# Weighted sums: the layout of the expanded blocks, of the transposed weights, and of the operand that the final products stream

## The chip, the cores and the metric

The kernel runs on one core of a Trainium2 chip. The metric is the time of one execution on the device in microseconds (us). The median of three runs is 10403.76 us (10387.06 to 10404.04).

## What is computed

Inputs are x and ctx of shape (32, 128, 1024) in fp32: 32 batch elements, 128 channels, 1024 points. Four layers follow one another. The first three are attention layers (chunked, with LoRA projections, chunked again); they give x3. The fourth finds, for each of the 1024 points, its 30 nearest neighbours among the points given by the first three channels of ctx, turns relative coordinates into features, sends these through a small network of three layers with batch norm, and ends so:

```
att = softmax(h[..., 0], axis=-1)                 # (B, 1024, 30)
xk  = x.transpose(0, 2, 1)[bidx, idx]             # rows of the 30 neighbours
agg = einsum('bnkc,bnk->bnc', xk, att)            # weighted sum of 30 rows
return x + agg.transpose(0, 2, 1)
```

(here C is 128). The change touches only the computation of `agg`.

## The kernel before

Most of the program is a loop over the 32 batch elements (attention layers, neighbour search, coordinates), followed by the network over all points. After that comes the stage of the weighted sums, again a loop over the 32 batch elements i. Within it every engine runs its own list of instructions, written out by hand, and semaphores alone order them against one another.

The stage gathers nothing. The weight with which source point m enters target point n is built as a product of one-hots. The index of a neighbour, 0 to 1023, is split by GpSimd into a high part l (0 to 15) and a low part (0 to 63), m = 64 l + low. There are 120 rows (4 groups of 30 neighbours) on the partitions and 256 columns of target points. Per batch element:

- `normalise` (L1451, VectorE) scales the attention; `transposes` (L753, TensorE) puts it into PSUM with the 120 rows on partitions.
- `weights` (L1463, VectorE), twice: for each l, BA[l] = (high part == l) times attention, an array of 16 x 128 per half.
- `blocks` (L1053, ScalarE), four times four operations: the expansion. For j = 0 to 3 it copies a quarter of BA, 1024 elements, into BD, scaled by `blockmask[:, j]`, which is 1 on the 30 rows of group j and 0 elsewhere. It runs in the order (h, p, l): it reads BA in steps of 128 elements (512 bytes), l innermost.
- `onehots` (L1472, VectorE), eight times: A1 = (low part == 0..63), 2048 elements.
- `chunk` (L766, TensorE), eight times: 32 products, each A1 (120 x 64, stationary) against 64 columns (l, j) of BD, into the PSUM buffer SCA or SCB. An fp32 product is two matmul records in the trace, so a chunk is 64 records.
- `columns` (L1061, ScalarE), eight times: the eviction of SCA or SCB, 128 x 1024, into WT, the transposed weights of half a batch element.
- `final` (L779, TensorE), twice: for each l and each half h of the partitions a product of X3D (64 x 128, stationary; rows of x3, loaded from DRAM) with the 256 columns (c, j) of WT at that l, accumulated over the 16 values of l in the PSUM bank PD (h = 0) or MISC (h = 1). Again 64 records.
- `finish` (L1486, VectorE) adds x3 and the result goes out over SyncE's queue.

BD, A1, SC, WT and X3D have two buffers each. The order on the engines: TensorE runs chunks 0 and 1, the second final of batch element i - 1, the transposes of i + 1, chunks 2 to 5, the first final of i, and chunks 6 and 7. ScalarE runs for v = 0 to 3 the blocks for the next pair of chunks, then the columns of chunks 2v and 2v + 1. VectorE runs one-hots 0 and 1, weights(1), one-hots 2 and 3, finish(i - 1), one-hots 4 and 5, weights(0) of i + 1, one-hots 6 and 7. A chunk waits for its one-hots (`a_done`), its blocks (`bd_done`) and the eviction of the chunk two before (`wt_done`). A one-hot waits for the chunk two before, since it overwrites its A1 (`chunk_ready`). `final` waits for the four evictions of its half.

The layouts before, innermost index last: BD is (h, p, l, j), so for one j the expansion writes in steps of 4 elements (16 bytes). The columns of a chunk's products are (l, j). WT is (l, c, j): the eviction reads PSUM straight and writes runs of 4 elements, and the 256 columns of one l lie side by side.

Of the kernel before, what the change touches and what calls it, by code (L numbers as in the profile page):

```python
# [25 lines left out]
GROWS = 4 * KNN  # L26
# [5 lines left out]
def program(nc, x_in, ctx_in, mask_in, w_in, b_qkv, w_out, wq, wk, wv, wo, at, bq, bk, bv, bo,  # L32
            mlp_k, consts, out, NB=B):
    f32, u32, bf16 = mybir.dt.float32, mybir.dt.uint32, mybir.dt.bfloat16
    ALU, ACT, AX = mybir.AluOpType, mybir.ActivationFunctionType, mybir.AxisListType
# [14 lines left out]
    with stack:  # L50
        def sb(name, shape, dt=f32):
            return stack.enter_context(nc.sbuf_tensor(name, shape, dt))

        def sem(name):
            return stack.enter_context(nc.semaphore(name))
# [24 lines left out]
        reg = sb("reg", [P, 3 * T + V1W + V2W])  # L80
# [50 lines left out]
        blockmask = con[:, 400:404]  # L131
# [17 lines left out]
        def pb(name, n):  # L149
            return stack.enter_context(nc.psum_tensor(name, [P, 512 * n], f32))  # L150
        SC = [pb("SCA", 2), pb("SCB", 2)]
# [44 lines left out]
        chunk_ready, wt_done, fin_ready, out_done = (sem(n) for n in (  # L196
            "chunk_ready", "wt_done", "fin_ready", "out_done"))
# [19 lines left out]
        def load_part(eng, q):  # L217
# [4 lines left out]
        LV, HV = 16, 64  # L222
        UC = 64
        free = arena[:, B * PAIRS:]
        BD = [free[0:GROWS, n * UC * 64:(n + 1) * UC * 64].rearrange("r (h p l j) -> r h p l j", h=2, p=32, l=LV)
              for n in range(2)]
        WT = [w.rearrange("p (l c j) -> p l c j", l=LV, j=4) for w in (free[:, 8192:12288], reg[:, 0:4096])]
        X3D = [w.rearrange("p (l c) -> p l c", l=LV) for w in (free[:, 12288:14336], kexp[:, :])]
        A1 = [gat[0:GROWS, n * 2048:(n + 1) * 2048].rearrange("r (h p c) -> r h p c", h=2, p=16) for n in range(2)]
        BA = [w[0:GROWS, :].rearrange("r (l c) -> r l c", l=LV) for w in (S01, pd01)]  # L230
# [30 lines left out]
        def settle(eng):  # L261

            eng.sem_inc(waited, 1)
# [164 lines left out]
        def _(pe):  # L428
# [3 lines left out]
            for n, (W, kc, w) in enumerate(WCHUNKS):  # L432
                if n >= 2:
                    pe.wait_ge(lora_done, n - 1)
                for c in range(0, w, 512):
                    last = mm(SC[n % 2][:, c:min(c + 512, w)], A_OF[id(W)][:, kc * P:(kc + 1) * P],
                              B_OF[id(W)][:, c:min(c + 512, w)], start=True, stop=True)
# [3 lines left out]
            for n in range(2):  # L441
                last = mm(MISC[:, n:n + 1], WL[n][:, 384:512], bL[:, n, 2:3], start=True, stop=True)
# [52 lines left out]
            with pe.Fori(0, NB) as i:  # L495
# [119 lines left out]
                for c in range(2):  # L615
                    for kc in range(KC):
                        last = mm(SC[1][:, c * P:(c + 1) * P], Wk[:, kc, c * P:(c + 1) * P], ctxT[:, kc, :],
                                  start=(kc == 0), stop=(kc == KC - 1))
                last.then_inc(k_ready, 1)
                for kc in range(KC):  # L620
                    last = mm(SC[1][:, 512:768], ctxT[:, kc, :], Wv[:, kc, :], start=(kc == 0), stop=(kc == KC - 1))
# [3 lines left out]
                for kc in range(KC):  # L625
                    last = nc.tensor.transpose(TP[:, kc * P:(kc + 1) * P], X1[:, kc * P:(kc + 1) * P], ident)
                last.then_inc(hT_ready, 1)
                pe.wait_ge(hT_evac, i + 1)
                for c in range(KC):
                    for kc in range(KC):  # L630
                        last = mm(SC[0][:, c * P:(c + 1) * P], Wq[:, kc, c * P:(c + 1) * P], hT[:, kc, :],  # L631
                                  start=(kc == 0), stop=(kc == KC - 1))
# [27 lines left out]
                for h in range(2):  # L660
                    for c in range(KC):
                        last = mm(SC[0][:, h * 512:(h + 1) * 512], OT[:, c * P:(c + 1) * P],  # L662
                                  Wo[:, c, h * 512:(h + 1) * 512], start=(c == 0), stop=(c == KC - 1))
# [7 lines left out]
                for t in range(NT):  # L671
                    last = nc.tensor.transpose(TP[:, t * P:(t + 1) * P], X0[:, t * P:(t + 1) * P], ident)
# [53 lines left out]
            with pe.Fori(0, NCH // 2 - 1) as i:  # L726
                for u in range(2):
                    n = i * 2 + u
# [9 lines left out]
            with pe.Fori(0, PARTS) as i:  # L738
                for u in range(PCH // 2):
                    n = i * (PCH // 2) + u  # L740
                    pe.wait_ge(a2_done, n + 1)
                    pe.wait_ge(h3_done, n + 1)
                    for h in range(2):
                        last = mm(SC[u % 2][0:G, h * CW:(h + 1) * CW], k3, act2[u % 3][0:GR, h * CW:(h + 1) * CW],
                                  start=True, stop=True)
# [11 lines left out]
            def chunk(i, c):  # L757
                v = c // 2
                pe.wait_ge(a_done, i * 8 + c + 17)
                if c % 2 == 0:  # L760
                    pe.wait_ge(bd_done, i * 4 + v + 5)
                pe.wait_ge(wt_done, i * 8 + c + 1)
                settle(pe)
                for p in range(16):
                    for h in range(2):
                        last = mm(SC[c % 2][64 * h:64 * h + 64, p * 64:(p + 1) * 64], A1[c % 2][:, h, p, :],  # L766
                                  BD[v % 2][:, h, c % 2 * 16 + p, :, :].rearrange("r l j -> r (l j)"),
                                  start=True, stop=True)
                last.then_inc(chunk_ready, 1)

            def final(i, par, k, half):
                pe.wait_ge(wt_done, i * 8 + 4 * half + 6)
                if half == 0:
                    pe.wait_ge(x3T_ld[par], k * 32 + 32)
                    pe.wait_ge(out_done, i + 2)
                settle(pe)
                for l in range(LV):
                    for h in range(2):
                        last = mm(FIN[h][:, half * 256:(half + 1) * 256], X3D[par][64 * h:64 * h + 64, l, :],  # L779
                                  WT[half][64 * h:64 * h + 64, l, :, :].rearrange("p c j -> p (c j)"),  # L780
                                  start=(l == 0), stop=(l == LV - 1))
                last.then_inc(fin_ready, 1)

            def aggregate(i, par, k, first=False, last=False):
                chunk(i, 0)
                chunk(i, 1)
                if not first:
                    final(i - 1, 1 - par, k - 1 + par, 1)
                if not last:
                    transposes(i + 1, 1 - par)  # L790
                for c in range(2, 6):
                    chunk(i, c)
                final(i, par, k, 0)
                chunk(i, 6)
                chunk(i, 7)
                if last:
                    final(i, par, k, 1)
# [13 lines left out]
        def _(act):  # L811
            A = nc.scalar.activation
# [35 lines left out]
            with act.Fori(0, NB) as i:  # L848
                if True:
# [90 lines left out]
                    for j in range(2):  # L940
                        last = A(halves[:, :, j, :], SC[1][:, 0:256].rearrange("p (c t) -> p c t", c=2), ACT.Copy,
                                 scale=pairmask[:, j:j + 1])
# [55 lines left out]
            with act.Fori(0, NCH // 2) as i:  # L998
                for u in range(2):
                    n = i * 2 + u  # L1000
                    act.wait_ge(l1_ready, n + NCH + 1)
                    act.wait_ge(l2_ready, n + 1)
                    for h in range(2):
                        last = A(S[u][0:GR, h * CW:(h + 1) * CW], SC[u][0:GR, h * CW:(h + 1) * CW], ACT.Identity,
                                 scale=gain[0:GR, h:h + 1], bias=shift[0:GR, h:h + 1])
# [41 lines left out]
            def blocks(i, v):  # L1047
                half, w = v // 2, v % 2
                act.wait_ge(ba_done, i * 2 + half + 5)
                act.wait_ge(chunk_ready, i * 8 + 2 * v + 2)  # L1050
                src = BA[half].rearrange("r l (h p) -> r h p l", h=2)[:, :, 32 * w:32 * w + 32, :]
                for j in range(4):
                    last = A(BD[v % 2][:, :, :, :, j], src, ACT.Copy, scale=blockmask[0:GROWS, j:j + 1])  # L1053
                last.then_inc(bd_done, 1)

            def columns(i, c):
                half = c // 4
                act.wait_ge(chunk_ready, i * 8 + c + 5)
                if c % 4 == 0:
                    act.wait_ge(fin_ready, i * 2 + half + 3)  # L1060
                A(WT[half][:, :, c % 4 * 16:c % 4 * 16 + 16, :].rearrange("p l c j -> p c l j"),  # L1061
                  SC[c % 2][:, :].rearrange("p (c l j) -> p c l j", l=LV, j=4), ACT.Copy).then_inc(wt_done, 1)

            def aggregate(i, last=False):
                for v in range(4):
                    if v < 3:
                        blocks(i, v + 1)
                    elif not last:
                        blocks(i + 1, 0)
                    columns(i, 2 * v)  # L1070
                    columns(i, 2 * v + 1)

            act.sem_inc(bd_done, 4)
            act.sem_inc(wt_done, 2)
            blocks(0, 0)
            with act.Fori(0, NB - 1) as i:
                aggregate(i)
# [520 lines left out]
```

## Time and profile before

| | |
|---|---|
| median of the runs | 10403.76 us |
| the profiled execution | 10408.93 us |
| its span, first to last instruction | 10407.0 us |
| busy: TensorE matmul | 7886.3 us (76%) |
| busy: VectorE | 7988.5 us (77%) |
| busy: ScalarE | 4010.1 us (39%) |
| busy: GpSimd | 511.4 us (5%) |
| mean granted TensorE clock | 0.764 of full speed |
| L1053, expansion | 512 operations, 534.9 + 538.0 us busy |
| L1472, one-hots | 256 operations, 583.0 us busy |

The shares are means over stages with different limits; what a change of one stage is worth has to be read inside that stage. In the groups the busy time of a line is a union in time, since operations of an engine overlap a little; the mean of one is from its start to its end. Idle time is shown with what released it. "reg", "arena", "kexp", "gat" are big SBUF tensors in which the arrays named above lie: BD in arena, WT in arena (first half) and reg (second half), A1 in gat, BA in S (first half) and pd (second half), X3D in arena and kexp.

### The profile page before, as it was taken

What the parts mean: (1) busy time and instruction counts of PE and PEld (TensorE: products, weight loads), DVE (VectorE), ACT (ScalarE), POOL (GpSimd) and SP (SyncE); (2) the same over time, 40 slices, a digit from 0 to 9 for tenths busy, and PEclk for the clock granted to TensorE, in tenths of its full rate; (3) what the DMA queues carried; (4) which work ended last, traced back from release to release, by engine and by line L of the source; (5) the groups of instructions that cost most, each with busy time, mean ns of one, the idle gap of its engine ahead of it and who ended that gap; (6) DMA issues with size and microseconds to landing.
All of it is one profiled execution on the core that took longest, in us unless ns stands there. A gap on an engine that the chain in (4) does not pass through costs nothing.

```text
span 10407.0 us, 195918 instructions
## 1 busy us (share of the span) xinstructions
PE 7886.3 (76%) x79424; PEld 5345.1 (51%) x79424; DVE 7988.5 (77%) x11226; ACT 4010.1 (39%) x4783; POOL 511.4 (5%) x776
## 2 busy tenths in 40 slices
PE   7777777777777777777777777777777775778888
PEld 4444444554544444545444444555554542277777
DVE  6887777788777877877777787787888785766666
ACT  2333333333233333333332332333332220499999
POOL 0000000000000000000000000000000000010000
PEclk8777777777777777777777777777777777889899
DMA  2111111111111111111111111111111113122222
GB/s 80 45 45 42 45 42 44 44 42 45 45 45 45 45 45 45 45 45 42 45 42 42 43 44 45 44 44 45 45 45 35 44 43 82 37 52 62 54 62 49
DMA packets 325409, 487.83 MB, mean 47 GB/s; under 512 B 133378, under 2 KB 246162, under 8 KB 323826
## 3 DMA queue, kind: packets, MB, share of 16 engines
q1 hardware_dynamic: 238269, 371.72, 11.6%
q10 hardware_dynamic: 86197, 102.55, 3.3%
q8 instruction: 712, 11.67, 0.5%
q14 instruction: 231, 1.89, 0.1%
HBM read 401.33 MB, written 72.88 MB: 46 GB/s over the span
## 4 chain that ended last, share of the span: by engine, by line
PE 46%; DVE 25%; ACT 15%; issue 12%; DMA 1%; DVEq 0%; ACTq 0%; SPq 0%; POOL 0%; POOLq 0%
ACT arena L1053 6%; PE PD L465 5%; PE PD L466 5%; PE SCA L662 5%; DVE m L1207 4%; PE SCA L631 3%; DVE pd L1213 3%; PE MISC L490 3%; PE TP L654 3%; PE SCA L506 2%; ACT S L859 2%; DVE mx L1258 2%; PE SCB L506 2%; DVE S L1252 2%; ACT kexp L892 2%
## 5 line engine op out<-in xcount | busy, mean ns | idle before, releaser
L1207 DVE MAX8 m<-pd 128x8 f32<-128x1024 f32 x1024 | 1251.2, 1222 | 316.4 <-ACT pd L834 160.5
L1211 DVE FIND_INDEX8 idx<-m,pd 128x8 uint32<-128x1024 f32 x1024 | 1248.4, 1219 | 9.6 <-issue 9.6
L506 PE MATMUL SCA<-con,S 128*128 128x128 f32 x1536 | 317.4, 374 | 1120.7 <-ACT S L859 1120.7
L1213 DVE MATCH_REPLACE8 pd<-m,pd 128x1024 f32<-128x1024 f32 x768 | 928.3, 1209 | 0.0
L506 PEld LDWEIGHTS SCA<-con,S 128*128 128x128 f32 x1536 | 249.1, 192 | 1187.7 <-ACT S L859 1187.7
L490 PEld LDWEIGHTS MISC<-ptab,gat 128*128 128x128 bf16 x23400 | 650.9, 101 | 363.6 <-issue 342.4
L1472 DVE TENSOR_TENSOR gat<-maskT,con 120x2048 f32<-120x2048 f32 x256 | 583.0, 2308 | 294.1 <-PE SCA L766 277.2
L465 PE MATMUL PD<-arena 128*128 128x512 f32 x1028 | 774.1, 846 | 43.6 <-ACT pd L834 25.7
L834 ACT ACTIVATE pd<-PD,xxcol 128x512 f32<-128x512 f32 x514 | 352.9, 686 | 1168.5 <-PE PD L466 1168.5
L859 ACT ACTIVATE S<-S 128x1024 f32<-128x1024 f32 x384 | 404.4, 1053 | 841.7 <-DVE S L1259 568.7
L466 PE MATMUL PD<-arena,con 1*128 1x512 f32 x1028 | 727.1, 793 | 0.0
L490 PE MATMUL MISC<-ptab,gat 128*128 128x24 bf16 x23400 | 673.5, 177 | 44.0 <-issue 26.8
L854 ACT ACTIVATE OT<-TP 128x256 f32<-128x256 f32 x384 | 147.1, 383 | 1301.9 <-PE TP L535 1301.9
L1241 DVE RECIPROCAL sm<-TP 128x16 f32<-128x16 f32 (+1 forms) x384 | 91.4, 238 | 620.2 <-PE TP L654 310.6
L506 PE MATMUL SCB<-con,S 128*128 128x128 f32 x1536 | 338.7, 393 | 275.1 <-ACT S L859 275.1
L1053 ACT ACTIVATE arena<-S,con 120x1024 f32<-120x1024 f32 x256 | 534.9, 2256 | 17.9 <-DVE S L1463 17.9
L1131 DVE TENSOR_TENSOR prod<-MISC,hm 128x480 f32<-128x480 f32 x390 | 405.6, 1040 | 173.0 <-PE MISC L490 173.0
L1053 ACT ACTIVATE arena<-pd,con 120x1024 f32<-120x1024 f32 x256 | 538.0, 2277 | 0.0
L662 PE MATMUL SCA<-arena,OT 128*128 128x512 f32 x1024 | 537.6, 691 | 0.0
L631 PE MATMUL SCA<-reg,arena 128*128 128x128 f32 x4096 | 494.3, 286 | 35.6 <-ACT reg L948 35.6
L631 PEld LDWEIGHTS SCA<-reg,arena 128*128 128x128 f32 x4096 | 488.2, 202 | 43.2 <-ACT reg L948 43.2
L766 PE MATMUL SCA<-arena,gat 120*64 120x64 f32 x8192 | 323.6, 248 | 237.5 <-ACT reg L1061 135.2
(260 smaller groups left out, 15328.8 us busy)
## 6 DMA issues: line engine op xcount, KB each, us to landing
gat<-low_scratch SPq DMA_DIRECT2D x396, 640.0 KB, 4.3
arena<-in_ctx ACTq DMA_DIRECT2D x33, 512.0 KB, 3.9
maskT<-in_mask ACTq DMA_DIRECT2D x32, 512.0 KB, 4.9
arena<-in_x ACTq DMA_DIRECT2D x32, 512.0 KB, 4.1
x_scratch<-arena ACTq DMA_DIRECT2D x32, 512.0 KB, 4.7
x3T_scratch<-arena ACTq DMA_DIRECT2D x32, 512.0 KB, 3.8
arena<-x3T_scratch SPq DMA_DIRECT2D x32, 512.0 KB, 7.1
arena<-x_scratch SPq DMA_DIRECT2D x32, 512.0 KB, 9.2
```

The lines of the kernel that those rows point to most:

```text
L465: mm(PD[:, :], ctx[:, t * P:(t + 1) * P], ctx[:, h * 512:(h + 1) * 512], start=True, stop=False)
L466: mm(PD[:, :], ones_row, xxrow[0:1, h * 512:(h + 1) * 512], start=False, stop=True).then_inc(pd_ready, 1)
L490: last = mm(place[:, o:o + 3 * NT], oh[n % NOH][:, kk * 256 + half * P:kk * 256 + (half + 1) * P], ptab[:, part, :, :].rearrange("p c t -> ...
L506: last = nc.tensor.transpose(SC[g % 2][:, b * 512 + j * P:b * 512 + (j + 1) * P], S[g % 2][:, b * 512 + j * P:b * 512 + (j + 1) * P], ident)
L631: last = mm(SC[0][:, c * P:(c + 1) * P], Wq[:, kc, c * P:(c + 1) * P], hT[:, kc, :], start=(kc == 0), stop=(kc == KC - 1))
L662: last = mm(SC[0][:, h * 512:(h + 1) * 512], OT[:, c * P:(c + 1) * P], Wo[:, c, h * 512:(h + 1) * 512], start=(c == 0), stop=(c == KC - 1))
L859: A(S[g % 2], S[g % 2], ACT.Exp, scale=scale).then_inc(exp_done, 1)
L1053: last = A(BD[v % 2][:, :, :, :, j], src, ACT.Copy, scale=blockmask[0:GROWS, j:j + 1])
L1207: step(V.max(m, buf[:, :]))
L1211: last = V.max_index(idx[:, t, 8 * r:8 * r + 8], m, buf[:, :])
L1213: step(V.match_replace(buf[:, :], m, buf[:, :], -3.0e38))
L1472: V.tensor_tensor(A1[c % 2], low[:, :, 16 * part:16 * part + 16].unsqueeze(3) .broadcast_to([GROWS, 2, 16, HV]), iota64[0:GROWS, :].unsque ...
```

## The change

BD becomes (h, p, j, l), and WT becomes (c, j, l). The columns of a chunk's products are then (j, l). The expansion reads as before and writes runs of 16 elements; the eviction reads and writes 1024 elements in one run; `final` takes its 256 moving columns at a step of 16 elements (64 bytes). Numbers of instructions, sizes, waits and their order stay as they are.

```diff
-        BD = [free[0:GROWS, n * UC * 64:(n + 1) * UC * 64].rearrange("r (h p l j) -> r h p l j", h=2, p=32, l=LV)
+        BD = [free[0:GROWS, n * UC * 64:(n + 1) * UC * 64].rearrange("r (h p j l) -> r h p j l", h=2, p=32, l=LV)
               for n in range(2)]
-        WT = [w.rearrange("p (l c j) -> p l c j", l=LV, j=4) for w in (free[:, 8192:12288], reg[:, 0:4096])]
+        WT = [w.rearrange("p (c j l) -> p c j l", l=LV, j=4) for w in (free[:, 8192:12288], reg[:, 0:4096])]
...
-                                  BD[v % 2][:, h, c % 2 * 16 + p, :, :].rearrange("r l j -> r (l j)"),
+                                  BD[v % 2][:, h, c % 2 * 16 + p, :, :].rearrange("r j l -> r (j l)"),
...
-                                  WT[half][64 * h:64 * h + 64, l, :, :].rearrange("p c j -> p (c j)"),
+                                  WT[half][64 * h:64 * h + 64, :, :, l].rearrange("p c j -> p (c j)"),
...
-                    last = A(BD[v % 2][:, :, :, :, j], src, ACT.Copy, scale=blockmask[0:GROWS, j:j + 1])
+                    last = A(BD[v % 2][:, :, :, j, :], src, ACT.Copy, scale=blockmask[0:GROWS, j:j + 1])
...
-                A(WT[half][:, :, c % 4 * 16:c % 4 * 16 + 16, :].rearrange("p l c j -> p c l j"),
-                  SC[c % 2][:, :].rearrange("p (c l j) -> p c l j", l=LV, j=4), ACT.Copy).then_inc(wt_done, 1)
+                A(WT[half][:, c % 4 * 16:c % 4 * 16 + 16, :, :].rearrange("p c j l -> p (c j l)"), SC[c % 2][:, :], ACT.Copy).then_inc(wt_done, 1)
```

Some lines outside the change are also shown below: L1131 multiplies a PSUM operand with `hm`, which it reads in steps of 240 two-byte elements (480 bytes); L1110 subtracts, reading `crd` in steps of 3 elements (12 bytes). L1176 and L1179 are two-input operations on contiguous arrays. L863 and L854 are ScalarE's plain copies from PSUM to SBUF.

## Rows read from the trace of the kernel before

**Rows 1.** Page: busy tenths of TensorE and ScalarE in 40 equal slices:

```profile
PE   7777777777777777777777777777777775778888
...
ACT  2333333333233333333332332333332220499999
```

**Rows 2.** By stretch: length; busy PE, PEld, DVE, ACT, POOL; clock; DMA:

```profile
9500.00:9900.00 400.00, 331.14 (x6419) 304.91 (x6416) 261.42 (x431) 399.16 (x241) 37.01 (x50) 0.91 0.25 58
...
9718.40:9723.00 4.60, 4.18 (x73) 4.03 (x75) 0.99 (x6) 4.60 (x3) 0.00 (x0) 0.50 0.02 7
...
9725.80:9733.00 7.20, 7.20 (x66) 6.20 (x66) 2.29 (x1) 7.20 (x5) 0.00 (x0) 1.00 0.01 2
```

**Rows 3.** Who waited for whom, 9500 to 9900: total us, times, longest:

```profile
PE SCA L766 <- ACT reg L1061: 46.4, 10, 5.1
...
ACT arena L1061 <- PE SCB L766: 0.8, 1, 0.8
```

**Rows 4.** Chain of waits, 9500 to 9900, shares by line:

```profile
by line: ACT arena L1053 43.9%; issue 19.6%; ACT reg L1061 8.2%; PE PD L779 6.9%; ACT arena L1061 6.2%; PE SCA L766 5.8%; PE SCB L766 5.0%; DVE gat L1472 1.7%; DVE S L1463 1.4%; ACTq L1058 0.4%; PE TP L753 0.4%; ACTq L1076 0.2%; PE MISC L77
```

**Rows 5.** Timeline, ScalarE: start, duration, engine, line, what, count, idle before:

```profile
9707.29 1.07 ACT L1061 ACTIVATE reg<-SCA 128x1024 f32<-128x1024 f32 x1
...
9709.15 8.31 ACT L1053 ACTIVATE arena<-S,con 120x1024 f32<-120x1024 f32 x4
...
9717.27 1.05 ACT L1061 ACTIVATE reg<-SCA 128x1024 f32<-128x1024 f32 x1
...
9747.23 1.09 ACT L1061 ACTIVATE reg<-SCA 128x1024 f32<-128x1024 f32 x1
```

**Rows 6.** Timeline, TensorE, 9709 to 9734:

```profile
9709.47 2.09 PE L766 MATMUL SCA<-arena,gat 120*64 120x64 f32 x64
...
9711.39 2.04 PE L766 MATMUL SCB<-arena,gat 120*64 120x64 f32 x64
...
9718.46 2.15 PE L766 MATMUL SCA<-arena,gat 120*64 120x64 f32 x35 [5.04 <-ACT reg L1061]
...
9722.52 3.29 PE L766 MATMUL SCB<-arena,gat 120*64 120x64 f32 x64
...
9725.74 0.48 PE L779 MATMUL PD<-reg,arena 64*128 64x256 f32 x1
...
9732.85 0.44 PE L753 MATMUL TP<-con,OT 128*120 128x128 f32 x2
...
9733.22 2.09 PE L766 MATMUL SCA<-arena,gat 120*64 120x64 f32 x64
```

**Rows 7.** Timeline, VectorE: one-hots (L1472) after chunks:

```profile
9711.72 4.49 DVE L1472 TENSOR_TENSOR gat<-maskT,con 120x2048 f32<-120x2048 f32 x2 [4.67 <-PE SCA L766]
```

**Rows 8.** Groups by shape, ScalarE: busy us, mean ns, idle before:

```profile
L1053 ACT ACTIVATE arena<-S,con 120x1024 f32<-120x1024 f32 x256 | 534.9, 2256 | 17.9 <-DVE S L1463 17.9
...
L863 ACT ACTIVATE ET<-SCA 128x1024 f32<-128x1024 f32 x192 | 196.5, 1023 | 232.5 <-PE SCA L506 232.5
...
L854 ACT ACTIVATE OT<-TP 128x256 f32<-128x256 f32 x384 | 147.1, 383 | 1301.9 <-PE TP L535 1301.9
...
L1061 ACT ACTIVATE reg<-SCA 128x1024 f32<-128x1024 f32 x64 | 69.0, 1078 | 2.5 <-PE SCA L766 2.5
```

**Rows 9.** Groups by shape, VectorE:

```profile
L1131 DVE TENSOR_TENSOR prod<-MISC,hm 128x480 f32<-128x480 f32 x390 | 405.6, 1040 | 173.0 <-PE MISC L490 173.0
...
L1176 DVE TENSOR_TENSOR X<-X 128x480 f32<-128x480 f32 x34 | 22.4, 659 | 1.2
...
L1110 DVE TENSOR_TENSOR OT<-crd,own 128x240 f32<-128x240 f32 x102 | 54.0, 585 | 4.2
...
L1179 DVE TENSOR_TENSOR X<-X,S 128x240 f32<-128x240 f32 x34 | 13.9, 408 | 1.2
```

**Rows 10.** Timeline: first expansions (ScalarE) and last addition (VectorE):

```profile
9111.88 16.23 ACT L1053 ACTIVATE arena<-S,con 120x1024 f32<-120x1024 f32 x8 [17.95 <-DVE S L1463]
...
10403.18 0.68 DVE L1486 TENSOR_TENSOR ET<-MISC,arena 128x512 f32<-128x512 f32 x1
```

## The prediction, made before the changed kernel ran

> **What bounds the kernel now.** I read the page's slices first. In 35 of the 40 slices (260 us each) the kernel runs parts that this change does not touch; in the last five, from about 9,100 us on, ScalarE's digit is 9 and TensorE's 7 to 8 [rows 1]. That last eighth is the stage of the weighted sums, the only one in which the three edited operations run. The table by stretch then gives ScalarE 399.2 of 400 us busy, TensorE 331 and VectorE 261 [rows 2]. Who waits for whom says the same: TensorE waits 46.4 us (of 400) for ScalarE's evictions at L1061, and ScalarE waits for TensorE hardly at all [rows 3]. The chain of waits has 43.9% of that stretch on L1053, ScalarE's block expansion, and only 6.9% on the final products [rows 4]. So the stage runs at ScalarE's pace, with TensorE at 83% close behind. ScalarE starts it at 9111.88 and the last addition ends at 10403.86 [rows 10].
>
> The pace: the same eviction recurs at 9707.29 and 9747.23, 39.9 us per batch element [rows 5]. Four expansions take 9717.27 - 9709.15 = 8.12 us, 2.03 each, and two evictions 1.86 us, 0.93 each [rows 5]. A batch element has 16 expansions and 8 evictions: 16 x 2.03 + 8 x 0.93 = 39.9 us.
>
> TensorE in the same time: chunk to chunk 1.92 us (9709.47 to 9711.39), so a pair of chunks is some 3.9 us; a final product from its first matmul to what follows is 9732.85 - 9725.74 = 7.11 us; the two transposes 0.37 us [rows 6]. Sum: 4 x 3.9 + 2 x 7.1 + 0.4 = 30.2 us. The rest of its 39.9 is waiting, and chunks at the lower clock after a wait: the stretch from 9718.4 was granted 0.50, that is 1.2 GHz, after 5.04 us of idling, and one chunk took 4.1 us there; a final product ran at 1.00 (2.4 GHz) [rows 2, 6].
>
> **The change part by part.**
>
> Expansions (512 in all). Reads stay at 512-byte steps; the writes go from 16-byte steps to runs of 16 elements. A plain ScalarE operation of 1024 elements takes 1.02 us, the expansion 2.26 [rows 8]. Which side costs the extra, the trace does not say for ScalarE, since no other operation of it is stepped. VectorE shows that stepped reads alone cost: L1131 (480-byte steps) takes 1040 ns where 480 plain elements take 659, 0.79 ns more per element; L1110 (12-byte steps) 585 where 240 plain take 408, 0.74 ns more [rows 9]. A plain element costs VectorE (659 - 408)/240 = 1.05 ns, so a stepped one costs 1.8 ns or 1.73 times. On ScalarE, whose plain element costs (1023 - 383)/768 = 0.83 ns [rows 8], this is 1.44 ns by the ratio or 1.8 by the time: an expansion of about 1.5 or 1.9 us where it is 2.03. Outer bounds are 0.9 (only the writes cost) and 2.03 (only the reads). I take 1.7. ScalarE then needs 16 x 1.7 + 8 x 0.88 = 34.2 us per batch element; it is 31 at 1.5, 37.4 at 1.9, and 21.4 and 39.5 at the outer bounds.
>
> Evictions (256). They read PSUM in order before and after; the writes go from runs of 4 to one run. L1061 takes 1078 ns against 1023 for the plain copy [rows 8]: 0.05 us off each, 0.4 us per batch element.
>
> Chunk products: same bytes, same contiguous moving operand of 64 columns. Nothing. The output columns only change order.
>
> Final products (64 of them, each of 64 matmul records of 256 columns). The moving columns go from contiguous to 64-byte steps. This is the part that decides, and the trace has no TensorE row with a stepped moving operand. One is 32 pairs of records, one for each of two banks, side by side: 7.11/32 = 0.22 us a pair [rows 6], 0.87 ns per column. Nearest rows are again the stepped reads of VectorE [rows 9]. If SBUF hands over a stepped word each 1.8 ns whoever asks, a final product takes 7.1 x 1.8/0.87 = 14.7 us; if it is the ratio, 7.1 x 1.73 = 12.3; if TensorE's fetch has slack for four-byte words, 7.1. I take twice, 14.2 us, nearer the first, because TensorE asks for its words faster than VectorE (0.87 ns against 1.05), which leaves it less slack, not more.
>
> One row is at odds with a rule of the Trainium skill, and it matters which holds. L1110 steps by 12 bytes and is slow [rows 9]. "SBUF — State Buffer", section "Door 1: The DMA port swizzle", has 16-byte lines, each of which wants two hits to be read at full speed, and calls fp32 steps up to four elements free; L1110 steps by three, so the rule is too kind. For the final products both speak against the change: a step of sixteen elements meets a new line at every column. The rule names no price for TensorE; as a doubling it would give the same 14.2 us.
>
> New pace. TensorE: 4 x 3.9 + 2 x 14.2 + 0.4 = 44.4 us. Then its chunks without a final product ahead of them wait for VectorE's one-hots: a one-hot may start 0.16 us after chunk c-2 (ended 9711.56, started 9711.72), takes 2.24 [rows 6, 7] and lets chunk c begin about 4.6 us after chunk c-2 began, where 3.9 would do: 0.7 us, and 0.3 more for its partner. Twice per batch element (chunks 4, 5 and the next 0, 1), 2 us. In sum 46.4 us against 39.9. ScalarE's 34 us (or 39.5) and VectorE's 26 [rows 2] lie beside it: its gain is off the path. In the last image the final product after chunk 7 is on the path as before, its doubling already counted. Batch elements: 32. 32 x 6.5 = 207 us. No transfer is made later than its user: with 14-us products the loads that follow a finished product have longer than now.
>
> The profiled execution took 10408.9 us (span 10407.0), 5 us over the median of the three runs, 10403.8. 10408.9 + 207 = 10616; on the median 10,611. I predict **10,610 us**. The case's own range: with 12.3-us products 42.6 us a batch element, 32 x 2.7 = +87, or 10,490 on the median; with 14.7 us 47.4, +240, or 10,644; with room for the waits between the engines 10,470 to 10,690.
>
> **Rivals.**
>
> A. TensorE reads the stepped columns at its usual pace or nearly. For it: at 0.87 ns per column these matmuls spend two cycles of 2.4 GHz on each, so a fetch that could deliver a word per cycle has slack. Against it: VectorE has no such slack to spare even at 1.05 ns a word [rows 9]. Then ScalarE's saving counts, down to TensorE's floor of 30.2 + 1.5 to 2 us, about 32. With an expansion of 1.7 us: 34.2, so -5.7 x 32 = -182: 10,220. With 1.9: 37.4, -80: 10,324. With 1.5 or less: 32, -253: 10,150. This also covers a product slowed by a third (9.5 us): 15.6 + 19 + 0.4 + 2 = 37 us, -93: 10,310. Break-even is 39.9 = 18 + 2F, F = 11 us, 1.55 times today's.
>
> The Trainium skill's "Vector Engine (DVE) Microarchitecture Reference", section "5.2 Measured stream behaviour on trn2", has writes at a small step the dearest (2.5 ns per column against about 1.7 for hops), which speaks for the larger saving; no row here shows stepped writes alone.
>
> B. The reads are the whole price of the expansion, and TensorE doesn't mind its steps. ScalarE still sets the pace at 16 x 2.03 + 8 x 0.88 = 39.5: -0.4 x 32 = -13 us, 10,391. Products at 1.55 times end here as well. No change that can be measured.
>
> C. TensorE pays much more than double, because two row groups read stepped at once: at three times 21.3 us, 15.6 + 42.6 + 0.4 + 2 = 60.6, +662: 11,070. Only the fact that no row excludes it speaks for it.
>
> **How the numbers follow.** Forecast case 0.50, A 0.38, B 0.08, C 0.04. A measurement of this kernel can tell about 0.2% (21 us) from no change. Faster by more: 0.38 (A). Within: 0.08 (B). Slower: 0.50 + 0.04. Both signs hold most of the chance, so the range spans them: from 10,140, below A's floor, to 10,700, above the forecast's upper end; outside are C and the extremes, about 0.1. Given the forecast case alone it is 10,470 to 10,690.
>
> **What would show it.** Right: in the profile after, the pitch of L779's pairs goes from 0.22 to some 0.43 us and a product takes 14 us; ScalarE's share in 9,200 to 10,300 falls from 100% to about 75%, TensorE's rises above 95%; L1053's mean falls from 2.26 to 1.6 to 2.0 us, L1061's to 1.02; TensorE waits for VectorE's one-hots in front of chunks 0, 1, 4 and 5, and no longer for L1061. Wrong: L779's pitch stays at 0.22 (A or B, told apart by L1053's mean), or the columns of L779 slow less than 1.55 times. Anything that moves before 9,100 us would be another cause altogether.

## The result: 3.0% slower, and what the profile after shows

The changed kernel takes 10714.24 us (median of 4, 10709.6 to 10716.11); the kernel before, run beside it, 10403.9 us. The ratio is 1.0301, with a 95% interval of 1.0283 to 1.0319. Measured again later beside other versions it was 1.0301 (1.0284 to 1.0318). So the sign is as forecast and the size is not: I forecast +2.0%, with 10,700 as the upper end of the range.

The slices of the page, against [rows 1]. Before 9,100 us nothing of note moved; the last six slices are the stage of the weighted sums, in which TensorE is now at 9 (8 in the first of them) and ScalarE has fallen from 9 to 7 and 8.

```profile
PE   7777777777777777777777777777777756899999
...
ACT  2333333333333333333233333333333304887787
```

Table by stretch (columns as in [rows 2]): TensorE is now busy 367 of 400 us (331 before), ScalarE 319 (399 before): 92% and 80%. The second row lies in a final product, the third and fourth in the pause and the slow chunk told of below; their clocks are 1.00, 0.86 and 0.50.

```profile
9500.00:9900.00 400.00, 367.05 (x5147) 242.25 (x5149) 206.94 (x347) 319.48 (x194) 29.60 (x40) 0.96 0.20 47
9724.40:9738.30 13.90, 13.90 (x66) 6.53 (x64) 5.53 (x8) 13.90 (x9) 3.70 (x5) 1.00 0.19 47
9742.40:9746.70 4.30, 0.00 (x0) 0.00 (x0) 4.30 (x11) 4.30 (x3) 0.00 (x0) 0.86 0.03 4
9746.70:9751.30 4.60, 3.63 (x63) 3.47 (x65) 1.54 (x8) 4.47 (x3) 0.00 (x0) 0.50 0.01 4
```

The timeline of TensorE, which answers to [rows 6]. A pair of final products starts each 0.43 us (9725.28 to 9725.72; 0.22 before), and a final product takes 9738.33 - 9724.35 = 13.98 us (7.11 before). Chunks are as before, 1.92 us apart where nothing keeps them. One of them waits 0.92 us for its one-hots.

```profile
9714.94 0.43 PE L753 MATMUL TP<-con,OT 128*120 128x128 f32 x2
...
9720.17 2.09 PE L766 MATMUL SCA<-arena,gat 120*64 120x64 f32 x64 [0.92 <-DVE gat L1471]
...
9724.35 0.68 PE L779 MATMUL PD<-arena 64*128 64x256 f32 x1
...
9725.28 0.60 PE L779 MATMUL PD<-arena 64*128 64x256 f32 x1
...
9725.72 0.60 PE L779 MATMUL PD<-arena 64*128 64x256 f32 x1
...
9738.33 2.09 PE L766 MATMUL SCA<-arena,gat 120*64 120x64 f32 x64
...
9746.75 2.15 PE L766 MATMUL SCA<-arena,gat 120*64 120x64 f32 x35 [4.47 <-issue]
9749.82 1.86 PE L766 MATMUL SCA<-arena,gat 120*64 120x64 f32 x29 [0.92 <-issue]
9751.37 3.73 PE L766 MATMUL SCB<-arena,gat 120*64 120x64 f32 x64
...
9769.11 0.43 PE L753 MATMUL TP<-con,OT 128*120 128x128 f32 x2
...
9815.53 0.44 PE L753 MATMUL TP<-con,OT 128*120 128x128 f32 x2
```

The transposes come once in a batch element, so they give the pace: 9815.53 - 9769.11 = 46.4 us, the forecast's number, but 9769.11 - 9714.94 = 54.2 us for the one before. The difference, 7.8 us, is in the three L766 rows of 9746 to 9755. TensorE stands still for 4.47 us and waits for nothing ("issue"), stops once more for 0.92 us after record 35 of the chunk, and runs both chunks at half clock. Such a pause comes 14 times between 9,130 and 10,620 us, 100 us apart, once in two batch elements. TensorE's loop runs 15 times, with two batch elements to a run, so it goes back to its start 14 times. That going back, with the slow chunks after it, is called a turn below. Over these 14 the batch element with the pause takes 52.8 to 54.6 us from transposes to transposes, 53.7 in the mean: a turn costs 7.4 us, and the one above is one of the dearer.

The trace shows what happens in the pause. In it lie two DMA packets of the kind "instruction", 16 KB each; they start at 9742.2 and 9742.7 and have landed at 9743.2 and 9744.9, and TensorE goes on 1.9 us later. A third lands at 9748.5, and the second stop ends 1.3 us after it. The view of DMA queues, 9742 to 9747 (packets, MB, share of the 16 DMA engines' time):

```profile
q8 instruction: 2, 0.03, 4.0%
```

The sum over the stage, from the first chunk to the end of the last addition: before 9120.12 to 10403.86, after 9108.65 to 10707.48, which is 315 us more. 32 x (46.4 - 39.9) = 208 and 14 turns x 7.4 = 104 make 312. The first chunk came 11 us earlier in this execution, through parts that the change does not touch; that is why the spans differ by 304 us only.

Groups by shape, against [rows 8]: the expansion went from 2.26 to 2.12 us, the eviction from 1.08 to 1.03.

```profile
L1053 ACT ACTIVATE arena<-S,con 120x1024 f32<-120x1024 f32 x256 | 518.5, 2115 | 18.0 <-DVE S L1462 18.0
...
L1061 ACT ACTIVATE reg<-SCA 128x1024 f32<-128x1024 f32 x64 | 65.8, 1028 | 80.0 <-PE SCA L766 80.0
```

### The profile page after: what moved, and what is told of

Same layout as the page of the kernel before. It is cut to its first block, busy times and chain, and to the rows that moved or that the text cites. A ratio compares the mean times of both kernels' runs of the same rounds, so it can differ in the third digit from the quotient of the medians.

```text
span 10710.6 us, 195918 instructions
## 1 busy us (share of the span) xinstructions
PE 8267.1 (77%) x79424; PEld 5324.0 (50%) x79424; DVE 7980.8 (75%) x11226; ACT 4009.3 (37%) x4783; POOL 511.4 (5%) x776
## 4 chain that ended last, share of the span: by engine, by line
PE 53%; DVE 27%; issue 11%; ACT 7%; DMA 1%; DVEq 1%; SPq 0%; POOL 0%; ACTq 0%; POOLq 0%
PE PD L779 8%; PE SCA L662 5%; PE PD L465 5%; PE PD L466 5%; DVE m L1206 5%; DVE pd L1212 4%; PE MISC L490 3%; PE SCA L766 3%; PE TP L654 3%; PE SCA L506 2%; PE SCA L631 2%; ACT S L859 2%; DVE mx L1257 2%; PE SCB L506 2%; DVE S L1251 2%
## 5 line engine op out<-in xcount | busy, mean ns | idle before, releaser
L854 ACT ACTIVATE OT<-TP 128x256 f32<-128x256 f32 x384 | 147.2, 383 | 1305.6 <-PE TP L535 1305.6
L1053 ACT ACTIVATE arena<-S,con 120x1024 f32<-120x1024 f32 x256 | 518.5, 2115 | 18.0 <-DVE S L1462 18.0
L1053 ACT ACTIVATE arena<-pd,con 120x1024 f32<-120x1024 f32 x256 | 521.6, 2120 | 0.0
L598 PE MATMUL TP<-reg,ET 128*64 128x34 f32 x8192 | 370.6, 255 | 167.0 <-DVE on L1241 167.0
```

The source lines that it names most:

```text
L1053: last = A(BD[v % 2][:, :, :, j, :], src, ACT.Copy, scale=blockmask[0:GROWS, j:j + 1])
```

## Experiments

### TensorE's part undone, ScalarE's kept (e1)

```diff
 # against the changed kernel
-        WT = [w.rearrange("p (c j l) -> p c j l", l=LV, j=4) for w in (free[:, 8192:12288], reg[:, 0:4096])]
+        WT = [w.rearrange("p (l m) -> p l m", l=LV) for w in (free[:, 8192:12288], reg[:, 0:4096])]
...
-                                  WT[half][64 * h:64 * h + 64, :, :, l].rearrange("p c j -> p (c j)"),
+                                  WT[half][64 * h:64 * h + 64, l, :],
...
-                A(WT[half][:, c % 4 * 16:c % 4 * 16 + 16, :, :].rearrange("p c j l -> p (c j l)"), SC[c % 2][:, :], ACT.Copy).then_inc(wt_done, 1)
+                A(WT[half][:, :, c % 4 * 64:c % 4 * 64 + 64],
+                  SC[c % 2][:, :].rearrange("p (m l) -> p l m", l=LV), ACT.Copy).then_inc(wt_done, 1)
```

> The changed kernel with only its TensorE part undone: the expansion reads in steps and writes runs of 16, chunk columns are (j, l), but the eviction reads PSUM in steps of 16 elements (64 bytes) and writes WT as (l, c, j), so the final products stream contiguous columns again. My theory: the slowdown is all TensorE's stepped columns, and the expansion's price lies in its reads. Then the pairs of final products are back at 0.22 us (product 7.1 us), L1053 stays at about 2.12 us mean, and ScalarE sets the pace: 16 x 2.02 + 8 x e, where e is the eviction. If stepped PSUM reads are free for ScalarE (e = 0.93) 39.8 us per batch element and 10,400 us; if they cost it as stepped SBUF reads do (e about 1.8) 46.7 us and 10,620. Rival (the slowdown sits in the new expansion or in the order of the chunk columns): the time stays near 10,710 with final products at 7.1 us.

Measured: 0.9984 of the kernel before (0.9973 to 0.9994), 10,367.7 us. Groups by shape of this version from 9,110 us on, with the final products' mean back at 0.38 us, as in the kernel before:

```profile
L1053 ACT ACTIVATE arena<-S,con 120x1024 f32<-120x1024 f32 x248 | 509.2, 2233 | 0.0
...
L779 PE MATMUL PD<-reg,arena 64*128 64x256 f32 x512 | 114.7, 379 | 0.0
...
L1061 ACT ACTIVATE reg<-SCA 128x1024 f32<-128x1024 f32 x64 | 72.8, 1137 | 4.2 <-PE SCA L766 4.2
```

So the whole slowdown goes with the way in which the final products read. Runs instead of steps in the expansion's writes brought next to nothing (2.23 against 2.26 us); the 2.12 of the changed kernel came in a stage in which the other engines had slowed down, which was not taken apart further. Evicting from PSUM at 64-byte steps costs nothing that the stage feels. From its start to its end an eviction is up to 0.1 us longer than before (1137 ns against [rows 8]'s 1078), but from one to the next it is 0.90 us, against 0.92 before; and e3 below, with the same stepped evictions and ScalarE less busy, has them at 1.02 us, as the changed kernel has its straight ones.

### Final products that read four words together (e2)

```diff
 # against the kernel before
-        WT = [w.rearrange("p (l c j) -> p l c j", l=LV, j=4) for w in (free[:, 8192:12288], reg[:, 0:4096])]
+        WT = [w.rearrange("p (c l j) -> p c l j", l=LV, j=4) for w in (free[:, 8192:12288], reg[:, 0:4096])]
...
-                                  WT[half][64 * h:64 * h + 64, l, :, :].rearrange("p c j -> p (c j)"),
+                                  WT[half][64 * h:64 * h + 64, :, l, :],
...
-                A(WT[half][:, :, c % 4 * 16:c % 4 * 16 + 16, :].rearrange("p l c j -> p c l j"),
-                  SC[c % 2][:, :].rearrange("p (c l j) -> p c l j", l=LV, j=4), ACT.Copy).then_inc(wt_done, 1)
+                A(WT[half][:, c % 4 * 16:c % 4 * 16 + 16, :, :].rearrange("p c l j -> p (c l j)"), SC[c % 2][:, :], ACT.Copy).then_inc(wt_done, 1)
```

> The kernel before, but WT is (c, l, j): the eviction is one straight run, and the final products take their 256 columns in runs of four elements (16 bytes) at steps of 64. Theory: TensorE pays for a single word away from its neighbour, not for a hop, so four together stream at full speed: pair of final products 0.22 us, ScalarE sets the pace with 16 x 2.03 + 8 x 0.88 = 39.5 us, time 10,390. Rival (anything not contiguous halves the stream): pairs at 0.43 us, time near 10,710.

Measured: 0.9999 (0.9987 to 1.0012); final products at 379 to 382 ns mean as before. Hops cost TensorE nothing when four words lie together. The eviction did not get cheaper by being one run (1070 to 1094 ns, 1058 to 1087 before), so the forecast's 0.05 us each was not there in this setting.

### What a step costs TensorE (e7)

```diff
 # against the changed kernel, put in words: columns that a final product streams, by l // 4 (w is the half's 4096 elements)
+half 0: w[0:256], step 2, step 3, step 4
+half 1: step 8, pairs at step 4, pairs at step 32, fours at step 32
```

> The changed kernel with other columns of WT streamed by the final products (so the weighted sums are of wrong numbers; amounts of work are the same): in the first half l = 0-3 contiguous, 4-7 at a step of 2 elements, 8-11 of 3, 12-15 of 4; in the second half l = 0-3 at a step of 8, 4-7 in pairs at a step of 4, 8-11 in pairs at a step of 32, 12-15 in fours at a step of 32. Theory A (a fetch brings 8 bytes, whose two words must both be wanted): 0.22 us a pair of matmuls for contiguous, pairs and fours, 0.43 for every single step of 2 and more. Theory B (16-byte lines, two hits each): step 2 at 0.22, step 3 in between, 4 and 8 at 0.43, pairs 0.22. Theory C (only contiguous is fast): everything else 0.43. The time as such says little: A about 10,500, B about 10,450, C about 10,660.

The timeline of TensorE. Each kind is eight pairs of records; the first block shows where the kinds of half 0 begin (contiguous, 2, 3, 4, and the chunk after), the second those of half 1 (8, pairs at 4, pairs at 32, fours, and the transposes after).

```profile
9738.22 0.48 PE L789 MATMUL PD<-arena,kexp 64*128 64x256 f32 x1
...
9740.05 0.39 PE L789 MATMUL PD<-arena,kexp 64*128 64x256 f32 x1
...
9741.86 0.49 PE L789 MATMUL PD<-arena,kexp 64*128 64x256 f32 x1
...
9744.57 0.62 PE L789 MATMUL PD<-arena,kexp 64*128 64x256 f32 x1
...
9748.30 0.51 PE L767 MATMUL SCA<-arena,gat 120*64 120x64 f32 x10
```

```profile
9719.71 0.70 PE L789 MATMUL PD<-reg,arena 64*128 64x256 f32 x1
...
9723.45 0.40 PE L789 MATMUL PD<-reg,arena 64*128 64x256 f32 x1
...
9725.28 0.37 PE L789 MATMUL PD<-reg,arena 64*128 64x256 f32 x1
...
9727.03 0.37 PE L789 MATMUL PD<-reg,arena 64*128 64x256 f32 x1
...
9728.86 0.43 PE L754 MATMUL TP<-con,OT 128*120 128x128 f32 x2
```

Divided by eight: contiguous 0.23 (0.22 without the start), step 2 0.23, step 3 0.34, step 4 0.47 (0.45 by the starts inside the kind), step 8 0.47; pairs at 4 0.23, pairs at 32 0.22, fours 0.23. That is theory B. Four fp32 words make 16 bytes: 256 words at a step of 3 lie in 192 such lines, 0.34 us or 1.77 ns a line; at a step of 4 in 256, 0.45 us or 1.76 ns; at a step of 2 in 128, which by that price is 0.225 us, about what the words themselves take (0.84 ns each). The step of 16 elements in the changed kernel, 0.43 us or 1.68 ns a line, is a little cheaper than the steps of 4 and 8, which no run takes apart. The time, 10,433 us (one run), is near theory B's 10,450. The rule of the Trainium skill ("SBUF — State Buffer", section "Door 1: The DMA port swizzle": two hits to a 16-byte line for full speed) holds for TensorE with fp32. Its remark that four fp32 elements are a free stride does not: a step of 4 already costs double.

### What a step costs ScalarE (e4 and e8)

```diff
 # e4, against the kernel before; BA's l innermost
-        BA = [w[0:GROWS, :].rearrange("r (l c) -> r l c", l=LV) for w in (S01, pd01)]
+        BA = [w[0:GROWS, :].rearrange("r (c l) -> r c l", l=LV) for w in (S01, pd01)]
...
-                src = BA[half].rearrange("r l (h p) -> r h p l", h=2)[:, :, 32 * w:32 * w + 32, :]
+                src = BA[half].rearrange("r (h p) l -> r h p l", h=2)[:, :, 32 * w:32 * w + 32, :]
...
-                    last = V.scalar_tensor_tensor(BA[half][:, l, :], Lf[par][:, cols], float(l), attT[par][:, cols],
+                    last = V.scalar_tensor_tensor(BA[half][:, :, l], Lf[par][:, cols], float(l), attT[par][:, cols],
```

> The kernel before with BA stored as (c, l) alone: the expansion reads one run and still writes at 16-byte steps. Theory (reads are the whole price and writes are free): L1053 at about 1.05 to 1.2 us, time as for the version that also writes runs, about 0.989 of the kernel before. Rival (a stepped write alone costs as much as a stepped read, and the two hide one another): L1053 stays at about 2 us and the time at that of the kernel before, 0.997 to 1.000 of it.

Measured: 0.9968 (0.9953 to 0.9983), L1053 at 2.22 us. A write at 16-byte steps alone costs nearly as much as both did (1.95 us from one expansion to the next, 2.04 before), and my theory that the writes were free fell.

```diff
 # e8, against the changed kernel, put in words: kinds of expansion by v
+v = 0: run -> step 4;  v = 1: step 2 -> runs;  v = 2: run -> runs;  v = 3: pairs at step 4 -> runs
```

> The changed kernel with four kinds of expansion in turn (the weighted sums are of wrong numbers; the elements moved are as many): v = 0 reads one run and writes at a step of 4 elements; v = 1 reads at a step of 2 and writes runs; v = 2 reads one run and writes runs; v = 3 reads pairs at a step of 4 and writes runs. Theory (16-byte lines, reads only): 1.05 us for v = 0, 2 and 3, and for v = 1, two words to a line, as well. Rival 1 (single words are dear whatever the line): v = 1 at 1.5 to 2.1. Rival 2 (writes cost too): v = 0 at 1.5 to 2.1. The time says nothing here, since TensorE's stepped products set it, about 10,700.

The timeline of ScalarE, the first expansion of each kind, v = 0 to 3:

```profile
9775.17 2.32 ACT L1065 ACTIVATE arena<-S,con 120x1024 f32<-120x1024 f32 x1
...
9738.47 1.23 ACT L1065 ACTIVATE arena<-S,con 120x1024 f32<-120x1024 f32 x1
...
9750.48 1.14 ACT L1065 ACTIVATE arena<-pd,con 120x1024 f32<-120x1024 f32 x1
...
9768.71 1.27 ACT L1065 ACTIVATE arena<-pd,con 120x1024 f32<-120x1024 f32 x1
```

Writes at 16-byte steps cost 2.32 us where runs cost 1.14; reads with two words to a line (1.23, 1.27) are near the full rate. Together with e1 (reads at 512-byte steps, written in runs: 2.23) and the kernel before (both: 2.26): either side at one word to a line sets the pace of about 2 ns an element, and a second one on the other side adds nothing. Rival 2 held. Time: 10,703.7 us, one run, or 1.031 of the kernel before as run beside it; the changed kernel has 1.030. Three quarters of the expansions at about half the price brought nothing: in the changed kernel ScalarE's work is off the path.

### The turn of TensorE's loop (e5)

```diff
-with pe.Fori(0, NB // 2 - 1) as pair:          # 15 turns
-    for odd in (1, 0):
-        aggregate(pair * 2 + (2 - odd), odd, pair + (1 - odd))
+with pe.Fori(0, (NB // 2 - 1) // 3) as trip:   # 5 turns
+    for q in range(3):
+        for odd in (1, 0):
+            aggregate(trip * 6 + (2 * q + 2 - odd), odd, trip * 3 + (q + 1 - odd))
```

> The changed kernel with TensorE's loop over pairs of batch elements written out three pairs to a turn: 5 turns in place of 15, all else the same. In the changed kernel TensorE stands still for about 4.5 us once in two batch elements, with nothing that it waits for, then runs two chunks at the lower clock. Theory: this is the loop's turn, which was hidden when ScalarE set the pace and now costs 54.2 - 46.0 = 8.1 us each time. Ten turns fewer: -81 us, 10,633. Rival (the pause has to do with a wait or with the power throttle, not with the turn): unchanged, 10,700 to 10,715, and the pauses stay 15.

Measured: 1.0229 (1.0212 to 1.0246), against 1.0301 for the changed kernel: 0.0072 x 10,390 = 75 us less, which the two intervals leave open by some 26 us either way; 81 were expected. In the traces, from the first transposes of the stage to the last, it is 65.5 us less. Who waits for whom on TensorE, 9,200 to 10,600 us, first the changed kernel, then this one:

```profile
PE SCA L766 <- issue: 76.6, 28, 5.1
PE SCA L766 <- DVE gat L1471: 38.7, 42, 1.0
```

```profile
PE SCA L766 <- DVE gat L1472: 63.0, 58, 3.6
...
PE SCA L766 <- issue: 4.8, 4, 1.5
```

The ten pauses went with the ten turns, and so did their chunks at half clock: the mean granted clock of 9,500 to 9,900 rose from 0.96 to 0.99. Smaller ones came up inside the written-out code, 8.4 us in all from the first transposes to the last, and 10 x 7.4 - 8.4 is about the trace's 65.5. At the four places where this loop still goes back to its start TensorE stands still for 3.2 to 3.6 us. The profile puts these waits down to one-hots, but the chunk at 9415.28 began 2.7 us after its one-hot was done (9410.31 + 2.29):

```profile
9410.31 2.29 DVE L1472 TENSOR_TENSOR gat<-maskT,con 120x2048 f32<-120x2048 f32 x1 [10.60 <-PE SCA L766]
...
9415.28 1.36 PE L766 MATMUL SCA<-arena,gat 120*64 120x64 f32 x35 [3.27 <-DVE gat L1472]
9417.70 1.86 PE L766 MATMUL SCA<-arena,gat 120*64 120x64 f32 x29 [1.06 <-issue]
```

Repeated, the changed kernel gave the value that the comparison needs:

> The changed kernel itself, again, on the same chip as the version above, so that the versions with thinned-out loops can be compared with it: 1.030 of the kernel before.

Measured: 1.0301 (1.0284 to 1.0318).

### Versions that beat both kernels (e3, e6, e9)

e3 puts e1's edit and e4's together: the expansion reads and writes runs, the final products stream contiguous columns, and VectorE writes in steps.

> The version with contiguous final products (expansion writing runs, eviction reading PSUM in steps) and BA stored as (c, l): VectorE writes its 32 x 128 weights of a batch element at 64-byte steps, and ScalarE's expansion reads 1024 elements in one run. Theory: the expansion's price was its stepped reads, so L1053 falls from 2.2 to about 1.05 us (0.9 from one to the next); ScalarE needs 16 x 0.9 + 8 x 1.0 = 22.4 us a batch element, VectorE's weights grow from 277 to some 370 ns each (+3 us, 29 in all), and TensorE sets the pace: 30.2 + 2 (one-hots) + 4 (half a loop turn) = 36.2, against 39.9. -3.7 x 32 = -118 us against the kernel before: 0.989 of it, 10,265 to 10,285. Rival (stepped work on any engine costs the same wherever it stands, so it only moves to VectorE or to its waits): no gain over the version before this edit.

Measured: 0.9865 (0.9848 to 0.9882), 10,247 us. L1053 fell to 1.14 us, VectorE's weights grew from 277 to 387 ns, and TensorE's waits are now for its turn and for one-hots, none for ScalarE. A batch element takes 33.1 us without a turn and 39.8 with one, 36.4 in the mean, as expected. Who waits for whom, 9,200 to 10,200 us:

```profile
PE SCA L766 <- issue: 64.0, 25, 4.9
PE SCA L766 <- DVE gat L1472: 42.9, 44, 3.4
PE SCB L766 <- DVE gat L1472: 7.7, 14, 0.6
```

e6 is e3 with e5's edit.

> The version in which the expansion reads and writes in runs and VectorE writes the weights in steps, with TensorE's loop written out three pairs to a turn (5 turns for 15). Theory: TensorE now sets the pace, so a turn is no longer hidden and costs about 8 us as it did in the changed kernel: ten fewer give -80 us beyond the version with 15 turns, 0.981 of the kernel before, about 10,190. Rival (VectorE's order of work sets the pace once ScalarE is fast): no difference between the two, both at 0.985 to 0.99.

Measured: 0.9836 (0.9817 to 0.9855): 30 us less than e3 for ten turns, not 80, and hardly clear of the two intervals. In the traces, from the first transposes to the last, it is 41 us; the parts ahead of the stage took 17 us more in the profiled execution of e6. In e3 a turn cost 6.7 us, so ten are 67. TensorE's waits of kind "issue" between 9,200 and 10,200 us fell from 64 to 26 us, but 15.3 of these stand in front of L779, inside the written-out code, where e3 had none, and 4.4 in front of chunks into SCB. The waits put down to one-hots rose from 51 to 64 us; 11 of these are three turns that are left, booked as in e5.

e9 is e6 with VectorE's loop written out in the same way.

> The fastest version so far (expansion and eviction cheap, contiguous final products, TensorE's loop three pairs to a turn) with VectorE's loop over pairs written out the same way. With TensorE's turns thinned out, TensorE still waited once for the one-hots for 3.6 us, at a chunk that follows VectorE's own turn. Theory: VectorE's turn is the next one behind, ten fewer of some 3 us give -30 us, 0.981 of the kernel before (the version without this edit had 0.9836). Rival: the waits for one-hots come from the order of the work (0.7 us a time, at every second pair of chunks) and not from the turn; the time stays at 0.9836.

Measured: 0.9838 (0.9822 to 0.9854). My theory fell: VectorE's turns are not what is behind. The waits put down to one-hots stayed (61 us, 64 in e6), and so did the long one of 3.6 us: it stands where TensorE's own loop goes back to its start, which I had taken for VectorE's turn.

## Why the prediction was right in its way and wrong in its size

- What bounds: right. ScalarE set the pace before, TensorE does after; the rivals A and B were decided by one number, the pace of stepped columns.
- Final products at 14.2 us: measured 14.0. The reason was half right, so the close number is in part luck. I carried over VectorE's 1.8 ns for a stepped word; TensorE paid 1.7 to 1.8 ns for a 16-byte line, and at a step of two words it does have slack (e7).
- The stated 2 us of waits for one-hots: measured twice 0.92 us, and 0.19 more for each partner. The sum of 46.4 us is what a batch element without a turn takes.
- **The step that failed: "32 x 6.5 = 207 us", the same cost for every batch element.** It left out the turn of TensorE's loop, once in two batch elements, 7.4 us by the profile and about 7.5 by e5 (75 us for ten). 14 x 7.4 = 104 us are the whole of the miss (10,714 against 10,610). [Rows 6] held a trace of it: the chunk at 9718.46 breaks off after 35 records. The 5.04 us of idling ahead of it is no sign by itself, since the wait at 9758.44, where no turn is, is as long. That the turn lay in the waits at its own places, the trace of the kernel before does show. A stop after record 35 comes ten times in it, each time where the loop goes back to its start. Each of the 14 waits at such places has an instruction packet in it, and none of the waits at the start of the other batch elements has one. And at 9799.33 the turn was not even hidden whole: TensorE began 1.1 us after the eviction that it is said to wait for had ended (9797.09 + 1.12):

```profile
9758.44 3.68 PE L766 MATMUL SCA<-arena,gat 120*64 120x64 f32 x64 [5.06 <-ACT reg L1061]
...
9797.09 1.12 ACT L1061 ACTIVATE reg<-SCA 128x1024 f32<-128x1024 f32 x1
...
9799.33 2.15 PE L766 MATMUL SCA<-arena,gat 120*64 120x64 f32 x35 [4.48 <-ACT reg L1061]
```

  I priced the wait as slack and never asked what else stood in it, nor what the chunks at half clock after it would cost once nothing waited for ScalarE.
- The shares: TensorE's was to rise above 95% and is 92% between 9,200 and 10,300 us, which is the same miss; ScalarE's was to fall to 75% and is 80%.
- The expansion at 1.7 us: wrong, 2.12 here and 2.23 with contiguous products. I took the stepped read on ScalarE to be between VectorE's ratio and VectorE's time; from one expansion to the next it is 2.0, above both, and the write side, which the change mended, did not add to it. It had no consequence for the time, since ScalarE was off the path (e8).
- With free columns the change would have been rival B, not A: e1 is at 0.9984. I gave A 0.38 and B 0.08; most of A rested on the 1.7.

## What to carry to other kernels

When the engine that sets the pace changes, everything that the old one covered comes due. Look on the next engine for idle time and slow stretches that recur at the loop's period, whatever the profile names as releaser, and price them before saying "the rest is slack". Mend a layout on both sides of an operation or not at all: a ScalarE operation that both reads and writes single words to a line keeps its price when one side is made contiguous; and put the steps where the engine has slack, here VectorE's 128-element writes.

## What the runs showed that I had not expected

- A TensorE turn cost 7.4 us in the changed kernel and 6.7 in e3: 4.5 to 5.1 us of pause in most, then two chunks at 1.2 GHz in place of 2.4. Writing the loop out brought 75 us in one version and 30 in another, where new pauses (up to 4.0 us) came up inside the written-out code.
- Both kinds of pause go with instruction packets of 16 KB. At a turn's pause TensorE goes on 1.8 to 2.9 us after one has landed (85 times in the twelve traces). The other stops with nothing to wait for are 150, and 148 of them end 1.2 to 1.6 us after one has landed, where 6 to 8% would by chance. So TensorE seems to wait for its instructions there. That is read from times alone: no run changed how instructions are loaded, and the trace does not name the engine that a packet is for.
- fp32 moving columns cost 0.84 ns a word or about 1.7 to 1.8 ns a 16-byte line, whichever is more, with two row groups running at once; pairs on one line stream at full speed at any hop tried (4 and 32 elements).
- ScalarE took 2.0 to 2.3 us for 1024 elements with one word to a line on its read side, its write side or both.
- ScalarE reading PSUM at 64-byte steps lost nothing from one eviction to the next (0.90 us for 1024 elements, 0.92 at unit steps).
